# Gated cross-attention and binarised feed-forward on one core: two early ScalarE jobs given to VectorE, with new orders on the engines

## The reference

```python
def xattn(query, key):
    a = jnp.einsum('bqd,bkd->bqk', query, key)
    return jnp.einsum('bqk,bkd->bqd', jax.nn.softmax(a, axis=-1), key)

def ffn(x, weight, bias):
    alpha = jnp.mean(jnp.abs(weight), axis=1, keepdims=True)
    return jnp.einsum('bsi,oi->bso', x, alpha * jnp.sign(weight)) + bias

x = x + jnp.tanh(g_xattn[0]) * xattn(layernorm(x), ctx_4096)
x = x + jnp.tanh(g_ffn[0]) * ffn(layernorm(x), weight, bias)
```

## Time and profile before

| What | Value |
|---|---|
| median of three runs | 985.3 us (984.62 to 986.54) |
| profiled execution, its own time | 985.79 us |
| span of the profiled execution | 984.0 us |
| TensorE matmul busy | 934.0 us (95%) |
| VectorE busy | 840.8 us (85%) |
| ScalarE busy | 589.3 us (60%) |
| GpSimd busy | 134.9 us (14%) |
| mean granted TensorE clock | 0.988 |

### The profile page before, as it was taken

How to read it: one execution, slowest core, us unless ns; L and a number is a source line. 1 busy time by engine, 2 the same in 40 slices (tenths; PEclk the granted TensorE clock), 3 DMA queues, 4 the chain that set the end, 5 groups by cost and what they waited for, 6 DMA issues and landing times.

```text
span 984.0 us, 14349 instructions
## 1 busy us (share of the span) xinstructions
PE 934.0 (95%) x5201; PEld 462.9 (47%) x5201; DVE 840.8 (85%) x1197; ACT 589.3 (60%) x655; POOL 134.9 (14%) x262
## 2 busy tenths in 40 slices
PE   1669999999999999999999999999999999999998
PEld 1445554444444444454444444444444445444443
DVE  6587799897888989899989979998989888889864
ACT  5999973856587573646657364745667464562320
POOL 0011020131001110203111220201102020111000
PEclk9779999999999999999999999999999999999999
DMA  9589747696897988787995959967797967765374
GB/s 332 181 233 229 225 128 199 179 202 112 185 218 154 217 158 221 150 177 168 217 239 97 242 121 237 196 144 202 165 230 125 240 137 152 196 128 102 65 177 186
DMA packets 365141, 178.66 MB, mean 182 GB/s; under 512 B 353424, under 2 KB 353424, under 8 KB 354448
## 3 DMA queue, kind: packets, MB, share of 16 engines
q1 hardware_dynamic: 365072, 177.76, 76.9%
HBM read 55.58 MB, written 33.55 MB: 91 GB/s over the span
## 4 chain that ended last, share of the span: by engine, by line
PE 69%; DVE 10%; issue 7%; ACT 5%; POOL 2%; DMA 2%; SPq 0%; ACTq 0%; DVEq 0%; POOLq 0%
PE y_ps L2621 53%; PE y_ps L2589 7%; PE c_ps L2569 5%; PE s_ps L2553 4%; DVE natural L1571 3%; ACT xn_q L952 1%; DVE xr L1656 1%; DMA xr<-in_x_dram 1%; ACT natural L933 1%; DMA ring_a<-natural 1%; ACT spare L1063 1%; DVE st L1661 1%; DVE snap_a L1689 0%; ACT xn_q L919 0%; DVE xr L1790 0%
## 5 line engine op out<-in xcount | busy, mean ns | idle before, releaser
L2621 PE MATMUL y_ps<-wsign,ring_a 128*128 128x512 fp8e4 x1792 | 400.6, 379 | 2.3 <-DMA ring_a<-natural 1.5
L2621 PEld LDWEIGHTS y_ps<-wsign,ring_a 128*128 128x128 f16 x1792 | 173.9, 98 | 209.8 <-DMA ring_a<-natural 2.8
L2621 PE MATMUL y_ps<-spare,ring_a 128*128 128x512 fp8e4 x896 | 202.8, 379 | 0.7 <-ACT snap_b L1087 0.7
L933 ACT ACTIVATE natural<-xn_a 128x1024 f16<-128x1024 f32 x76 | 79.5, 1053 | 109.2 <-DVE xn_a L1803 49.9
L2621 PEld LDWEIGHTS y_ps<-spare,ring_a 128*128 128x128 f16 x896 | 87.3, 98 | 105.8 <-issue 1.5
L952 ACT ACTIVATE xn_q<-xr,nm,r 128x1024 f32<-128x1024 f32 x62 | 76.8, 1238 | 68.7 <-POOL nm L791 34.3
L1571 DVE TENSOR_TENSOR natural<-xn_a,natural 128x1024 f16<-128x1024 f32 x78 | 94.7, 1216 | 10.9 <-ACT natural L933 10.9
L1571 DVE TENSOR_TENSOR natural<-xn_q,natural 128x1024 f16<-128x1024 f32 x64 | 78.1, 1220 | 25.3 <-ACT natural L933 25.0
L2621 PE MATMUL y_ps<-sg,ring_a 128*128 128x512 fp8e4 x448 | 99.4, 379 | 0.0
L1656 DVE SCALAR_TENSOR_TENSOR xr<-c_ps,coef,xr 128x512 f32<-128x512 f32 x104 | 77.6, 746 | 21.5 <-PE c_ps L2569 21.1
L2569 PE MATMUL c_ps<-kd,pt 128*128 128x512 f16 x256 | 79.7, 394 | 11.5 <-DVE xr L1656 8.6
(11 more groups left out here) (121 smaller groups left out, 1001.4 us busy)
## 6 DMA issues: line engine op xcount, KB each, us to landing
xr<-in_x_dram SPq DMA_DIRECT2D x32, 1024.0 KB, 6.2
out_dram<-xr SPq DMA_DIRECT2D x30, 1024.0 KB, 5.1
spare<-n_L_ffn_weight_real_dram SPq DMA_DIRECT2D x8, 1024.0 KB, 7.3
ctx_f<-in_ctx_dram SPq DMA_DIRECT2D x8, 512.0 KB, 6.6
xr<-n_L_ffn_weight_real_dram SPq DMA_DIRECT2D x4, 1024.0 KB, 5.0
ctx_f<-n_L_ffn_weight_real_dram SPq DMA_DIRECT2D x4, 1024.0 KB, 7.3
out_dram<-xr SPq DMA_DIRECT2D x8, 256.0 KB, 2.2
ring_a<-natural SPq DMA_TRANSPOSE x102, 4.5
```

The source lines that it names most:

```text
L933: nc.scalar.activation(natural[:, i % RN, 0, :], src, ACT.Copy).then_inc(high_set, 1)
L2621: last = nc.tensor.matmul(y_ps[:, BANKS[j] + n, :], ring_a[:, slot_a(p, j), part, k, :], RIGHT[j][:, k // 2, chunk(n), k % 2], start=(firs ...
```

## The change

Two settings are changed. VectorE takes the absolute sums of weight tiles 1, 3 and 5 (`TENSOR_REDUCE` with absolute values, straight from the stage), and `ROWS_DVE` is 2, so for tile 1 ScalarE writes the high half from `xr` and VectorE the f32 rows. Then the lists of TensorE, VectorE, ScalarE, the sync engine and the table `NAT` are written in a new order over the whole kernel; GpSimd's list too. Apart from the three `sum_abs` calls, which go from ScalarE's list to VectorE's, every list holds the same calls as before.

```diff
-    ABS_DVE = ()
+    ABS_DVE = (1, 3, 5)
...
-        ROWS_DVE = 1
+        ROWS_DVE = 2
...
             load_x(0)
             load_keys(0)
+            load_gates()
+            load_w(1)
             load_w(0)
-            load_w(1)
...
-                    ("q", 6, 0), ("A11", 0, 0),
-           ("q", 6, 1), ("A12", 0, 0), ("S3", 0, 0),
+                    ("q", 6, 0), ("q", 6, 1),
+           ("A11", 0, 0), ("A12", 0, 0), ("S3", 0, 0),
```

More of the change, by code:

```diff
@@ L1104, in _ @@
             sum_abs(2)
+            sign(3)
+            exp(0)
             sum_rows1(2)
-            exp(0)
+            copy_pt(0)
             square_rows1(2)
-            copy_pt(0)
-            sign(3)
+            take_w(0)
             direct_high_q(2, 0)
             sign(4)
-            take_w(0)
+            take_w(1)
             direct_high_q(2, 1)
+            direct_high_x1(0, 0)
+            exp(1)
+            sum_rows1(3)
+            copy_pt(1)
             sign(5)
-            exp(1)
-            take_w(1)
-            direct_high_x1(0, 0)
-            copy_pt(1)
-            sum_rows1(3)
             direct_high_x1(0, 1)
@@ L1932, in _ @@
-            spread_alpha(11)
-            make_t2(0)
-            take_w(7)
-            make_n4(0)
-            attention(4, 3)
-            add_bias(3)
+            spread_alpha(9)
+            attention(3, 2)
+            add_bias(2)
+            spread_alpha(10)
+            attention(3, 3)
+            take_w(6)
+            make_t1(0)
+            finish_y(2, 0)
+            spread_alpha(11)
+            attention(4, 0)
+            take_w(7)
+            spread_alpha(12)
+            take_alpha(2)
@@ L2114, in _ @@
-            attention(13, 2)
+            low_a(3, "S1")
+            attention(13, 0)
+            add_bias(11)
+            key_max(2)
+            attention(13, 1)
+            finish_pair(3, "C11", 0)
+            low_a(3, "A22")
+            low_q(14, 0)
+            attention(13, 2)
+            low_q(14, 1)
+            finish_pair(3, "C11", 1)
+            attention(13, 3)
+            make_s4(3)
+            finish_pair(3, "C22", 0)
+            low_a(3, "S4")
             key_scales(2)
-            low_a(3, "S4")
@@ L2319, in _ @@
-            make_s1(9)
-            split_probs(24)
-            make_s2(9)
-            low_q(25, 0)
-            low_a(9, "S2")
+            finish_pair(8, "C22", 1)
+            low_keys(3)
+            finish_pair(8, "C21", 0)
+            low_a(9, "A11")
+            make_s3(9)
+            finish_pair(8, "C21", 1)
+            finish_pair(8, "C12", 0)
+            low_a(9, "A12")
+            low_q(25, 0)
+            make_s1(9)
+            finish_pair(8, "C12", 1)
+            low_a(9, "S3")
@@ L2746, in _ @@
             plain_block(3, 3, 0)
+            scores(6)
             plain_block(3, 3, 1)
@@ L2750, in _ @@
             half_product(0, 0, 0, 0)
-            scores(6)
+            transpose_probs(6)
             half_product(0, 0, 0, 1)
+            attend(6, 0)
             half_product(0, 0, 1, 0)
@@ L2755, in _ @@
             half_product(0, 1, 0, 0)
-            transpose_probs(6)
             half_product(0, 1, 0, 1)
-            attend(6, 0)
             half_product(0, 1, 1, 0)
             half_product(0, 1, 1, 1)
+            attend(6, 1)
             half_product(0, 2, 0, 0)
+            scores(7)
             half_product(0, 2, 0, 1)
-            attend(6, 1)
-            scores(7)
             attend(6, 2)
@@ L2799, in _ @@
             half_product(1, 1, 1, 0)
+            half_product(1, 1, 1, 1)
             attend(8, 1)
-            half_product(1, 1, 1, 1)
             half_product(1, 2, 0, 0)
+            attend(8, 2)
             half_product(1, 2, 0, 1)
-            attend(8, 2)
+            attend(8, 3)
             half_product(1, 2, 1, 0)
@@ L2809, in _ @@
             transpose_probs(9)
-            attend(8, 3)
             half_product(1, 3, 0, 1)
@@ L2818, in _ @@
             half_product(1, 4, 0, 1)
+            attend(9, 3)
             scores(10)
-            attend(9, 3)
             half_product(1, 4, 1, 0)
@@ L2868, in _ @@
             half_product(2, 6, 0, 1)
-            transpose_probs(12)
             half_product(2, 6, 1, 0)
-            attend(12, 0)
             half_product(2, 6, 1, 1)
@@ L2914, in _ @@
             half_product(4, 0, 1, 0)
-            scores(15)
             attend(14, 0)
@@ L2977, in _ @@
             attend(17, 2)
+            scores(18)
             half_product(5, 4, 0, 1)
@@ L2981, in _ @@
             half_product(5, 4, 1, 1)
-            scores(18)
             half_product(5, 5, 0, 0)
@@ L3021, in _ @@
             half_product(6, 4, 1, 1)
-            scores(20)
             half_product(6, 5, 0, 0)
@@ L3030, in _ @@
             half_product(6, 6, 1, 1)
-            transpose_probs(20)
+            scores(20)
             half_product(7, 0, 0, 0)
@@ L3059, in _ @@
             half_product(7, 4, 0, 1)
-            scores(22)
             half_product(7, 4, 1, 0)
@@ L3064, in _ @@
             half_product(7, 5, 0, 1)
+            scores(22)
             half_product(7, 5, 1, 0)
@@ L3078, in _ @@
             half_product(8, 1, 0, 1)
+            scores(23)
             attend(22, 1)
-            scores(23)
             half_product(8, 1, 1, 0)
@@ L3182, in _ @@
             half_product(10, 5, 0, 0)
+            scores(28)
             half_product(10, 5, 0, 1)
             half_product(10, 5, 1, 0)
-            scores(28)
             half_product(10, 5, 1, 1)
@@ L3227, in _ @@
             half_product(11, 6, 0, 1)
+            transpose_probs(30)
             half_product(11, 6, 1, 0)
             half_product(11, 6, 1, 1)
-            scores(30)
+            attend(30, 0)
             half_product(12, 0, 0, 0)
```

1425 lines of the change are left out of this document (701 added, 724 removed), and 40 rows, old and new, of the table NAT.

## The result

The changed kernel takes 993.7 us (median of 4 executions, 992.4 to 997.0) against 985.5 (median of 4): a ratio of 1.0088, with a 95% interval of 1.0061 to 1.0114. It is slower by 8.2 us. "No change" was wrong, and so was the range of 981.0 to 988.2 around the forecast of 984.5. The profiled execution was the slowest of the four: 996.97 us, of which 995.1 are span, so it is set against before's 985.79 and 984.0.

A forecast was written before the change was run, and what follows sets the result against it. Bound: start of the sign-product stream, unchanged work and the stream's waits. Terms: -0.6 (start) + 0.6 (new wait) - 0.64 (152 us) = -0.6 us, so 985.3 - 0.6 = 984.7, rounded to 984.5; range 981.0 to 988.2.

The forecast's parts named there:

- What bounds the kernel: Whole kernel: end is the first sign product's start (71.61 us before), unchanged work, and the few waits in that stream.
- The steps in the head: Before the first sign product: exponential at 35.7 us, tile 0's aggregate 48.4, tile 2's scores end 66.7, later order losing that gain.
- rival 2: Head: the gates' load lands late, at 14.9 us, context rows start 2.5 us late; 987.2 us, chance 0.12.
- the better of the two ways: Head, tile 2's scores: TensorE back at 2.4 GHz, so these take 2 us less with the turn before them.
- The term of the start: First sign product between 70.4 and 72.1 us, taken as 71.0: a gain of 0.6 us.
- rival 1: ScalarE's relief carries through: first sign product at 67.4 to 69.5 us, smaller waits behind; 981.7 us, chance 0.33.
- The new wait: Just behind the first sign product: TensorE waits 0.6 us for ScalarE's copy of tile 2's probabilities.
- the one at 152 us: TensorE's wait for the spreading of the last absolute sums, 0.64 us, counted as gone.
- The other waits: Further on in the stream: some 6.9 us of waits from coincidences of one order, their mean left unchanged.
- Rival 3: Stream over 800 us: the new order meets worse coincidences, waits grow by half, 3.5 us; 988.2 us, chance 0.13.
- Two of my own signs of being wrong: First product before 69.5 or after 73 us; waits in the stream differing by more than 3 us from before.
- The place where page and trace were weighed: Head, GpSimd's chain for the x1 scale: held under VectorE, up to 1 us costs nothing, 1.56 us costs 0.6.

The follow-up runs named there:

- `early_new`: The changed order and settings up to about 255 us, the order of before from there, against the kernel before: 990.7 us, ratio 1.0053.

## Why the prediction was wrong

**What bounds the kernel** was right and held in the profiles: the start of the stream plus the waits in it. With the settings alone, too, the earlier start is lost to waits in the stream. A lag made at one place was still there hundreds of us later, to a few tenths.

**The steps in the head** were right in direction. The first exponential came at 34.8 us (35.7 predicted), the aggregate of tile 0 at 47.1 (48.4), the gates' tanh at 11.43 with `kd` at 15.15, so that rival 2 did not occur, the three sums at 2.3 us each. The clock was the better of the two ways that I had left open, as the scores of tile 2 in 1.95 us instead of 2.72 show. They ended at 63.2 us, where I had 66.7, or 64.7 with the clock back. The order behind them then cost more than I had: 6.0 us to the end of the copy into `ring_a` instead of 5.2 (3.7 before). The first sign product was at 69.36 us, outside 70.4 to 72.1, and in the other nine profiles with this head at 67.3 to 69.8 (with before's head at 70.8 to 71.6). The term of the start was mis-sized: 0.6 for 2.25 us. Half clock on its first 8 matmuls, which I had not thought of, gave 1.6 back (in two of the other nine profiles it did not occur), so that the net of the step was as small as predicted, by luck and for another reason. The start lies within the 67.4 to 69.5 us of rival 1, but the relief did not carry through: the settings alone showed that a start 3.1 us earlier can be worth nothing at 178 us.

**The new wait** at tile 2's first attend chunk was 0.41 us (0.6 predicted), and the one at 152 us is gone, as predicted.

**"The other waits [...] Their mean I leave as it is": this is the step that failed.** They went from 7.1 to 15.5 us, with 3.0 us of half clock. Nothing in the work or in the shares after 150 us had changed, and I took that as a ground for an unchanged mean. It is none. The kernel before had an order in which few of these coincidences occurred, and the same work in another order had twice as much of them. Rival 3 named the mechanism, with a chance of 0.13 and 3.5 us. The waits grew by 8.4 us, more than twice that, and it priced a wait by its length alone and left the clock out, another 3.0. Its share of 88% for VectorE was no measure either: the two costliest waits began with GpSimd, which is busy for 14%. Two of my own signs of being wrong came true: a first product before 69.5 us, and waits that differ by more than 3 us.

**The place where page and trace were weighed** failed with it. The row was read right, a GpSimd operation held under a VectorE one with two inputs, but I tried it at one place in the head and wrote that it "does not move the sum". It had to be applied to every VectorE instruction of that kind that had moved; the longest, 4.42 us, had moved from 138.7 to 214.7 us, next to a mean on ScalarE's path. The Trainium skill, GPSIMD Engine Reference, "Key points", states the contention, and the trace agrees: 4.45 us for an operation of 0.24. The hold ended with the VectorE instruction, and with the first quarter when the instruction was in quarters (1.25 us).

What stays open: why the half clock followed a given wait in one execution and not in another, what exactly ends the earlier start's gain at 100 to 106 us when only the settings change, and why the second wait of `early_new` was so short in its profile.

## What to carry to other kernels

When a stream on one engine is full, a new order of the same work is not neutral: look through the places where a short operation on its path comes to stand behind a long or waiting one, on its own engine or, for GpSimd, under a long two-input VectorE instruction, and count a long wait with the half clock that may follow it. The long elementwise instruction off the critical path was better issued in pieces, at 0.2 us, than moved as a whole. A gain at the head is worth what is left of it at the next point where another resource paces the stream, so measure it there and not at the first product.

## What the runs showed of the hardware

A GpSimd operation on one column lasted until the end of the VectorE fp8 subtraction that it met: 4.45 and 3.26 us beside one instruction of 4.42, 1.25 beside its quarters. It is not always one instruction: at 795.76 us of the changed kernel such an operation took 3.22 us, under two VectorE instructions with two inputs in a row (1.16 and 2.28 us).

Behind its waits TensorE's matmuls were sometimes at half clock for some us and sometimes not, even at the same place of the same program. Behind the wait at 240 us the profiled execution of the change had 8 matmuls in 3.18 us; the repeated run, behind the same 3.30 us, 8 in 3.57 and 1.3 us more lost on the ten behind them; behind 1.85 us at 440 us, 8 took 1.89. Behind the 2.05 us at 293 us 16 matmuls took 5.30 us in one execution and 3.62 in the other (granted clock 0.61 and 1.00):

```profile
293.62 5.30 PE L2621 MATMUL y_ps<-spare,ring_a 128*128 128x512 fp8e4 x16
```

```profile
293.70 3.62 PE L2621 MATMUL y_ps<-spare,ring_a 128*128 128x512 fp8e4 x16
```
